# Tokens placed by expert and rank in four groups while attention and the first expert tiles run

## The reference

```python
x = x + xattn(layernorm(x), ctx, ctx)      # x, ctx: 16 batches x 256 tokens x 256
# gates = [q, k, v] @ kernel + bias; log_D = cumsum(log_sigmoid(f)) differences + i, causal
# D = exp(log_D - rowmax); C = (q k^T / sqrt(32)) * D; h = C / max(|sum C|, exp(-rowmax)) @ v
# 8 heads of 32; then layernorm over each head, times outnorm_weight
x = x + ffn(layernorm(x), w12, w3, gate_w)
# scores = x @ gate_w^T; top 2 of 8 experts, softmax over the two
# hidden = silu(x w1_e^T) * (x w2_e^T); y = sum over the two of prob * hidden @ w3_e^T
```

## Time and profile before

| what | value |
|---|---|
| median of 3 runs | 655.55 us (653.4 to 657.51) |
| the profiled execution | 654.9 us, span 653.1 us, mean granted clock 0.933 |
| busy share PE / PEld / DVE / ACT / POOL | 86% / 71% / 69% / 53% / 45% |
| DMA | 73.44 MB, mean 112 GB/s |

### The profile page before, as it was taken

How to read it: one execution, slowest core, us unless ns; L and a number is a source line. 1 busy time by engine, 2 the same in 40 slices (tenths; PEclk the granted TensorE clock), 3 DMA queues, 4 the chain that set the end, 5 groups by cost and what they waited for, 6 DMA issues and landing times.

```text
span 653.1 us, 14222 instructions
## 1 busy us (share of the span) xinstructions
PE 564.8 (86%) x3612; PEld 466.0 (71%) x3613; DVE 451.9 (69%) x987; ACT 348.5 (53%) x769; POOL 296.5 (45%) x312
## 2 busy tenths in 40 slices
PE   3779879999989951239999999999999999999993
PEld 1334668888878840127888888888888888888882
DVE  4664586787777778946667677667767767767762
ACT  2456556777777755014555555555555555555551
POOL 5423136365455534032555555555555555555532
PEclk9899998999999955559999999999999999999998
DMA  7875336787776668921433333333333333433322
GB/s 231 252 225 162 91 93 185 200 212 197 210 219 172 193 161 244 279 50 17 66 50 50 62 51 50 62 52 50 62 52 50 59 54 49 59 55 49 59 40 24
DMA packets 66018, 73.44 MB, mean 112 GB/s; under 512 B 12762, under 2 KB 55776, under 8 KB 65984
## 3 DMA queue, kind: packets, MB, share of 16 engines
q0 software_dynamic: 18240, 28.17, 25.1%
q1 hardware_dynamic: 38528, 36.21, 19.1%
q10 hardware_dynamic: 9216, 8.65, 3.9%
HBM read 43.51 MB, written 19.01 MB: 96 GB/s over the span
## 4 chain that ended last, share of the span: by engine, by line
issue 40%; POOL 15%; PE 14%; DVE 14%; DMA 10%; ACT 4%; SPq 1%; ACTq 0%; DVEq 0%; POOLq 0%
POOL xg L1168 9%; DMA out_rows<-ys,index 6%; PE bank L1287 5%; POOL out_rows L1177 4%; PE dots L1269 3%; DVE ohn L996 2%; DMA w12h<-in_x 2%; DVE ohp L995 2%; DVE c L846 1%; DVE st L727 1%; PE dots L1222 1%; ACT x2n L636 1%; PE bank L1336 1%; PE dots L1220 1%; DVE tot L887 1%
## 5 line engine op out<-in xcount | busy, mean ns | idle before, releaser
L1177 POOL DMA_INDIRECT out_rows<-ys,index x71 | 112.5, 1585 | 156.1 <-DVE ys L1048 145.1
L1054 DVE TENSOR_TENSOR w3l<-w,w3h 128x1024 fp32r<-128x1024 f32 x71 | 87.2, 1229 | 30.9 <-issue 29.7
L1168 POOL DMA_INDIRECT xg<-token_table,index x71 | 70.4, 992 | 46.1 <-DVE index L1013 24.4
L693 ACT CAST w3h<-w 128x1024 fp32r x71 | 74.4, 1048 | 20.4 <-issue 20.4
L1409 PE MATMUL bank<-w3l,hth 128*128 128x256 f32 x284 | 76.5, 302 | 1.8 <-DVE w3l L1054 1.8
L1410 PE MATMUL bank<-w3h,hth 128*128 128x256 f32 x284 | 70.8, 282 | 0.0
L1287 PE MATMUL bank<-aug,c 128*128 128x99 f32 (+2 forms) x512 | 63.9, 279 | 6.0 <-DVE c L846 5.9
L1287 PEld LDWEIGHTS bank<-aug,c 128*128 128x128 f32 x512 | 60.8, 195 | 11.0 <-DVE c L846 10.3
L1048 DVE TENSOR_SCALAR ys<-bank,pc 128x256 f32<-128x256 f32 x71 | 34.4, 484 | 46.6 <-PE bank L1413 46.6
L1031 DVE TENSOR_TENSOR htl<-bank,hth 128x512 fp32r<-128x512 f32 x71 | 49.1, 692 | 25.2 <-ACT hth L683 25.2
L1381 PE MATMUL weighs<-w12l,xh 128*128 x144 | 62.3, 432 | 1.1 <-DVE xl L1020 1.1
(11 more groups left out here) (172 smaller groups left out, 1235.1 us busy)
## 6 DMA issues: line engine op xcount, KB each, us to landing
w12l<-in_w12T SPq DMA_DIRECT2D x24, 256.0 KB, 3.5
aug<-in_ctxv SPq DMA_DIRECT2D x16, 264.0 KB, 3.5
w12h<-in_x SPq DMA_DIRECT2D x16, 256.0 KB, 3.6
w12l<-in_ctxT SPq DMA_DIRECT2D x16, 256.0 KB, 3.6
qbd<-w12h SPq DMA_DIRECT2D x64, 64.0 KB
x<-in_x SPq DMA_DIRECT2D x16, 256.0 KB, 3.3
out_rows<-x ACTq DMA_DIRECT2D x16, 256.0 KB, 2.5
token_table<-x2n ACTq DMA_DIRECT2D x16, 256.0 KB, 3.5
```

Of the source, the lines that this page charges most:

```text
L693: nc.scalar.copy(W3H[i][:], w3[:, bass.ds(e, 1)].rearrange("p a k d -> p (a k d)")).then_inc(w3h_ready, 1)
L1054: v.tensor_tensor(W3L[i][:], w3[:, bass.ds(e, 1)].rearrange("p a k d -> p (a k d)"), W3H[i][:].bitcast(F32), ALU.subtract).then_inc(w3l_re ...
L1168: q.indirect_dma_start(out=XG[x][:], out_offset=None, in_=table, in_offset=bass.IndirectOffsetOnAxis(ap=index[:, j:j + 1], axis=0)).then_i ...
L1177: q.indirect_dma_start(out=out, out_offset=bass.IndirectOffsetOnAxis(ap=index[:, j:j + 1], axis=0), in_=YS[o][:], in_offset=None, compute_ ...
```

## The change: what it does

- The tokens are routed in four groups of batches (0 to 2, 3 to 6, 7 to 11, 12 to 15). A group's top two, ranks (by matmul, with the counts of earlier groups) and slots are computed at the end of VectorE's steps two to four after the group's last batch. A slot is (expert, rank), at a fixed place of a table in memory, `slot_table`. GpSimd writes a token's number and probability there by one indirect DMA per block and choice (`place`): 64 of 128 x 8 bytes. 28 are in attention, 36 in the expert tiles, at most one or two a tile after the first.
- Three lists of tiles (21, 20 and 30) are made from it: counts, row numbers, an indirect read of up to 32 table rows (`fetch_list`), three transposes on TensorE, and copies to `index`, `prob`, `etab`, `clear`. The first list needs seven batches and is made in step 15, the second at tile 16, the third at tile 33. The one-hot products go.
- Instructions on VectorE: `largest` 6 for the first choice and 5 for the second, `chosen` 4, `take_ranks` 1 or 2, `slots` 3, `chances` 3; for a list `counts` 7 (13 the first time), `list_rows` 8 and `take_list` 6. `ranks` is 8 to 12 small matmuls.
- The rest of attention's rows (the last two batches' residual, normalisation and scores, the last group's routing) is done in tiles 0 to 11 (`remains`).
- VectorE's row statistics come after the second `combine` of a step, and scores, routing and `free_low` after them. SP loads the values ahead of the residual rows. The squares get a buffer of their own.
- All 16 steps are written out, as are the first 36 tiles (on VectorE all).
- The eight late pieces of w12 are split in steps 4 to 8, two a step: one low part by accumulating DMA, one on VectorE. Those of the last three batches are subtracted on VectorE.
- w3 isn't kept in SBUF: SP loads 512 KB for each tile into one of two buffers, two tiles ahead, once `w3l` has freed it. The register loads of the expert on ScalarE and VectorE, and `pc`, go.
- The slot table is filled early by a copy from memory to memory (264 KB).

The hunks below, after the constants: SP's loads in the expert tiles, ScalarE's `remains`, VectorE's steps and `remains`, GpSimd's placements and lists, TensorE's steps and `remains`.

```diff
+GROUPS = ((0, 3), (3, 7), (7, 12), (12, B))
+CUTS = (7, 12, B)
+FULL = [-(-(c * S * TOPK - NE * (P - 1)) // P) for c in CUTS[:2]]
+LISTS = ((0, FULL[0]), (FULL[0], FULL[1]), (FULL[1], TILES))
...
+    def load_w3(j, i):
+        wait(sp, w3l_ready, j - 1)
+        e = sp.value_load(etab[0:1, bass.ds(j, 1)], min_val=0, max_val=NE - 1)
+        sp.dma_start(W3[i][:], w3T[:, bass.ds(e * (KH * E), KH * E)]).then_inc(w3_in[i], 16)
...
+    sp.wait_ge(tables, 1)
+    load_w3(0, 0)
+    load_w3(1, 1)
+    load_rows(B - 1, 1)
+    for j in range(UNROLLED):
+        if j + 2 == FULL[0]:
+            sp.wait_ge(tables, 2)
+        load_w3(j + 2, j % 2)
+        if j == 0:
+            sp.sem_inc(may_add, 1)
+        elif j < 3:
+            sp.wait_ge(y_added[1 - j % 2], 16)
+            sp.sem_inc(may_add, 1)
+        else:
+            order(j, j % 2)
...
+        if j == 0:
+            turned(B - 3)
+        if j == 1:
+            squares(B - 1)
+        if j in (2, 5, 9):
+            nc.scalar.preload_act_table_set("natural_log_exp_and_others")
+        if j == 2:
+            row_scales(B - 2)
+            head_scales(B - 1)
+        if j == 3:
+            normal_rows(B - 2)
+            store_rows(B - 2)
+        if j == 4:
+            turned(B - 2)
+        if j == 5:
+            row_scales(B - 1)
+        if j == 6:
+            normal_rows(B - 1)
+            store_rows(B - 1)
+        if j == 7:
+            turned(B - 1)
+        if j == 9:
+            odds(len(GROUPS) - 1)
...
+    for b in range(B):
+        i = b % 2
+        if has(b, 1):
+            far(b - 1)
+        combine(b, 0)
+        if b == 2:
             columns(1, bank[7])
+        if has(b, 1):
+            centre(b - 1)
+        for gr, (lo, hi) in enumerate(GROUPS[:-1]):
+            if b == hi + 4:
+                take_ranks(gr, RANKS)
+        combine(b, 1)
+        if b == B - 1:
+            take_list(0, RANKS)
+        if b == 0:
             preactivation(1)
             maxima(1)
+        if has(b, 1):
+            variances(b - 1)
+        if has(b, 2):
+            row_statistics(b - 2)
+        if b == 1:
             three_parts(dve, v, negM, REST, m_parts, 2 * PARTS - 1, 0, PARTS)
+        if has(b, 3) and b < B - 1:
+            take_scores(b - 3, SCORES)
+        for gr, (lo, hi) in enumerate(GROUPS[:-1]):
+            if b == hi + 2:
+                largest(gr, 0)
+            if b == hi + 3:
+                largest(gr, 1)
+                chosen(gr)
+            if b == hi + 4 and b < B - 1:
+                slots(gr)
+        if has(b, 2):
+            row_means(b - 2)
+        for gr in range(2):
+            if b == GROUPS[gr][1] + 4:
+                chances(gr)
+        if b == GROUPS[1][1] + 5:
+            counts(0)
+        if b == GROUPS[1][1] + 6:
+            list_rows(0)
+        if FREE_AT < b <= FREE_AT + FREE_STEPS:
+            free_low(b - FREE_AT - 1)
...
+        if j == 0:
+            slots(2)
+            chances(2)
+            centre(B - 1)
+        if j == 1:
+            take_scores(B - 3, bank[7][:, 0:NC * NE])
+            row_statistics(B - 2)
+        if j == 2:
+            variances(B - 1)
+            counts(1)
+        if j == 3:
+            mix(B - 1)
+        if j == 4:
+            row_statistics(B - 1)
+        if j == 5:
+            take_scores(B - 2, bank[7][:, 0:NC * NE])
+            list_rows(1)
+        if j == 8:
+            take_scores(B - 1, bank[7][:, 0:NC * NE])
+            largest(3, 0)
+        if j == 9:
+            largest(3, 1)
+            chosen(3)
+        if j == 10:
+            take_ranks(3, FINAL)
+            slots(3)
+        if j == 11:
+            chances(3)
+        if j == 16:
+            take_list(1, bank[7])
+        if j == 20:
+            counts(2)
+        if j == 21:
+            list_rows(2)
+        if j == 33:
+            take_list(2, bank[7])
+    last_low(B - 3)
+    last_low(B - 2)
+    take_scores(B - 4, SCORES)
+    last_low(B - 1)
     low(0, 0)
+    far(B - 1)
+    take_ranks(2, RANKS)
...
+    def place(g, lo, hi):
+        k0 = group(g)[2]
+        pool.wait_ge(slots_ready, g + 1)
+        pool.wait_ge(pairs_ready, g + 1)
+        for k in range(k0 + lo, k0 + hi):
+            q.indirect_dma_start(out=places, out_offset=bass.IndirectOffsetOnAxis(ap=slot[:, k:k + 1], axis=0),
+                                 in_=pairs[:, k, :], in_offset=None).then_inc(placed, 16)
+    def fetch_list(ph):
+        w = LANES
+        pool.wait_ge(row_ready, 2 * ph + 2)
+        pool.wait_ge(placed, 16 * TOPK * NC * CUTS[ph])
+        q.indirect_dma_start(out=listed[0:w].rearrange("p s c -> p (s c)"), out_offset=None, in_=place_rows,
+                             in_offset=bass.IndirectOffsetOnAxis(ap=rowid[0:w, ph:ph + 1], axis=0)
+                             ).then_inc(list_in, 16)
...
+        if b in (8, 9, 10):
+            place(0, 4 * (b - 8), 4 * (b - 7))
+        if b == 11:
+            place(1, 0, 2)
+        if b in (12, 13):
+            place(1, 5 * b - 58, 5 * b - 53)
+        if b == 14:
+            place(1, 12, 16)
...
+        if j == 0:
+            place(2, 0, 4)
+        if 1 <= j < 4:
+            place(2, 2 * j + 2, 2 * j + 4)
+        if 4 <= j < 14:
+            place(2, j + 6, j + 7)
+        if j == 14:
+            fetch_list(1)
+        if 15 <= j < 31:
+            place(3, j - 15, j - 14)
+        if j == 31:
+            fetch_list(2)
...
+        for gr, (lo, hi) in enumerate(GROUPS[:-1]):
+            if b == hi + 4:
+                pe.wait_ge(kvb_ready, HG * (b + 1))
+                ranks(gr, bank[6][:, 384:512])
+        if has(b, 3):
+            turn_rows(b - 3)
+        if b == 2:
+            pe.wait_ge(o1_taken, 2)
+            columns(1, bank[7])
+        exponents(b, i, 1)
+        values(b, i, 0)
+        scores_(b, i, 1)
+        pe.wait_ge(kvb_ready, HG * (b + 1))
+        if b == B - 1:
+            pe.wait_ge(rank_taken, 2)
+            turn_list(0, bank[6][:, 384:512])
...
+    def remains(j):
+        if j == 0:
+            turn_rows(B - 3)
+        if j == 1:
+            route(B - 3, bank[7], 0)
+        if j == 4:
+            pe.wait_ge(score_ready, B - 2)
+            turn_rows(B - 2)
+        if j == 5:
+            route(B - 2, bank[7], 0)
+        if j == 7:
+            pe.wait_ge(score_ready, B - 1)
+            turn_rows(B - 1)
+        if j == 8:
+            route(B - 1, bank[7], 0)
+        if j == 10:
+            pe.wait_ge(score_ready, B)
+            ranks(3, FINAL)
+        if j == 16:
+            pe.wait_ge(rank_taken, 4)
+            turn_list(1, bank[7])
+        if j == 33:
+            pe.wait_ge(tables, 2)
+            turn_list(2, bank[7])
+        if j == UNROLLED - 1:
+            pe.wait_ge(tables, 3)
     pe.wait_ge(tables, 1)
+    route(B - 4, bank[6], NH * DV)
+    pe.wait_ge(o0_taken, B)
+    rows(0, 0)
     pe.wait_ge(w_lo, W1)
     for i in range(2):
+        pe.wait_ge(added[i], ADDED[i])
+    pe.wait_ge(free_added, 16 * FREE_STEPS)
+    pe.wait_ge(free_lo, FREE_STEPS)
+    pe.wait_ge(last_lo, SOLO)
+    pe.wait_ge(score_ready, B - 3)
+    ranks(2, bank[6][:, 384:512])
```

1039 lines of the change are left out of this document (551 added, 488 removed).

## The result

The changed kernel takes 689.73 us (median of four, 679.14 to 694.67) against 655.38 (653.40 to 657.51) before. The ratio is 1.043, with a 95% interval of 1.030 to 1.055: slower, where 628 was forecast. Kernels that carry the routing in attention scatter by 2% from run to run, so of these a median is read with its range, and a profile by its landmarks.

What follows compares the result with a forecast made beforehand. Attention was taken as a chain with TensorE in most links, the expert tiles as TensorE busy without a break. Tile 0 at 249.0 + 6.65 + 338.3 + 15 + 17.9 = 626.9, plus 1.8: 628.7, said as 628; range 610 to 646.

Steps and rivals of the forecast that it cites:

- the attention end moves by -10 + 19 + 1.4 + 1 = +11.4: Attention: new order, VectorE's additions, rank products and the slot table's early copy together move its end to 237.8 us.
- I take -10: Attention: row statistics moved into VectorE's idle time ahead of `tot` save 10 us; bounds 0 to -13.4, or -18.
- The routing on VectorE, "+16" of the +19: Attention: routing instructions lengthen VectorE's steps, 48 x 0.25 = 12.0 plus 21 x 0.207 = 4.3 us.
- The late pieces: Attention steps 4 to 8: weight-piece casts and negation on ScalarE 0, at worst 6; VectorE's `free_low` subtractions 3.0 us.
- The first list's 2.5: Attention step 15: list fetch behind the last four placements delays `turn_list` and values by 2.5 us (0 to 5).
- The handover's sum: Attention's end to tile 0: VectorE's work 8.7 plus 2.5 for the first list, 11.2 us, tile 0 at 249.0.
- The tiles' +15: Expert tiles: moved routing and remaining rows add 15 us by the largest engine excess per tile; bounds 6 and 26.
- The clock: Rival, attention: TensorE's pauses drop its clock to 1.2 GHz, five half steps 3.1 us longer; 643 us; chance 0.12.
- The W3 ring: Rival, expert tiles: 512 KB W3 loads land later than 6.75 us and lengthen all tiles; 669 us; chance 0.07.
- GpSimd becomes the bound: Rival: placements at 1.9 us cost +13 in attention, +5 in tiles, expert changes hold adds; 646 us; chance 0.15.
- More is hidden: Rival: tile additions cost 6, first list comes in time, new order gives 18; 612 us; chance 0.16.
- The rule on the port: Attention: by the skill's VectorE-GpSimd lock, each of 28 placements could wait out a VectorE instruction; nothing in the sum.

Runs made afterwards that it cites:

- b_dve: Kernel before, in its own order, with 81 small unused VectorE instructions (stand-ins for the routing) added in attention steps 5 to 15; 675.6 us.
- a_old: Changed kernel with attention's order taken back to that of before, rows' mean ahead of the routing; routing, placements and late pieces stay; 676.4 us.
- a_k: a_old_mid with TensorE's rank product behind the second scores and the late weight pieces one a step ahead of ScalarE's row scales; 670.0 us.
- a_nb: Changed kernel with the rows' mean (`nb`) moved directly behind the row statistics, ahead of the routing's instructions; 686.3 us.
- a_old_mid: a_old with the early placements behind their step's mix, ahead of the state's input, instead of at the step's end; 668.7 us.
- b_order: Kernel before with only the new order: row statistics behind the second product, ScalarE's row scales behind the head scales; 663.7 us, ratio 1.012.
- b_place64: Kernel before with only 64 plain GpSimd scatters of 8 bytes a row added, 28 in attention and 36 in expert tiles; 677.5 us.

## Why the prediction was wrong, step by step

**The step that failed** is "the attention end moves by -10 + 19 + 1.4 + 1 = +11.4". It moved by +56.5. Two of its terms are now measured apart. *"I take -10" for the new order* is +7.7. The idle 1.18 us of VectorE was real, but it was no slack for the statistics: put there, they make ScalarE's `x2n` late, and ScalarE, whose queue I did not follow past `nb`, then holds `tot`. For instructions that nobody waits for it was slack, as b_dve shows. *The routing on VectorE, "+16" of the +19* for 69 instructions, comes out in the old order (19.4 for the stand-ins, 72 of which count), but by two errors that cancel: 27.3 us of instructions, longer than I had them, less what hides in idle time. In the new order the stand-ins cost 43 to 44. That nothing hides there is what the prediction itself says ("the idle time is then spent"); it lacked the longer form beside GpSimd's mix and the clock.

Order and stand-ins together, without a placement or a weight piece, end at 276 to 277 of the 281.6. This is not 51 of the 56.5 us explained, since the parts don't add up (taking the late pieces away gives 8.0, moving `nb` 17.5). And the stand-ins are stretched more often than the real routing. In the changed kernel the routing's 72 instructions from step 4 to the last product are busy 22.3 us, where I had 16.3 with their gaps, and the four `free_low` 4.3 for 3.0; only 14 of the 72 took over 0.4, against 46 of the stand-ins. In the old order the two prices measured apart, 19.4 for the additions and 20.2 for the placements, make 39.6, and a_old, which has both and the rest, ends 37.5 later than before.

**The other terms of attention.** The late pieces, "taken at 0, at worst 6" on ScalarE and 3 on VectorE: 8.0 when left out of the changed kernel, give or take the scatter, so the bounds held and the middle did not. `ranks` waiting for `kvb` was not changed by itself; its two waits are 9.4 us together in the changed kernel, far over my +1.4, but a_k, in which the rank product stands elsewhere, was no faster. GpSimd in attention: 3 us for 28 placements in the new order, which fits "it stays level", but 20.2 in the old one. The first list's 2.5 is hidden when attention is slow and is 6.7 when it is not (a_nb).

**What held, and what was luck.** The placement took 1.35 for 1.3, and W3 landed after 3.8, under the 6.75 that costs nothing. The handover's sum, 11.9 for 11.2, is in part luck. The 2.5 for the first list were not there; in their place VectorE waited for ScalarE's cast of one of the last weight pieces, and its subtraction took 1.75 instead of 0.69:

```profile
290.88 1.75 DVE L1099 TENSOR_TENSOR w12l<-w12l,w12h 128x512 fp32r<-128x512 f32 x1 [1.82 <-ACT w12h L689]
```

The tiles' +15 was meant for all of them and is 26. That tiles 0 to 10 alone take 16.0 over is luck too: they hold waits for the landing of adds, as the 3.80 above, which I had at nothing, and in the kernel with the old order 6 of their 18.4 go with the W3 loads.

**The rivals.** *The clock* was a right mechanism, with a chance of 0.12 and 15 us for five half steps, far too few: a mean of 0.84 from 110 to 230 us is some 38 of 120 us at 1.2 GHz. It comes with the waits: behind 3.12 and 1.64 us of them, and behind 5.07, the next values took 3.71 and 3.63. By the section of the Trainium skill that I cited (TensorE: Matmul & The Clock Gate), idle gaps take the clock back; the trace agrees, with 0.84 over attention against 1.00. *The W3 ring* had the right load and the wrong place: the tiles hardly wait for W3's landing, yet its loads cost 18 to 21 us. *GpSimd becomes the bound* is false in the tiles without W3 loads, where 36 placements cost 0.0; in attention its sign, statistics waiting for `x`, came in the old order at 1.35 per placement, not 1.9. *More is hidden* is false, and its sum was wrong: an order worth 18 instead of 10 gives 8, not 5, so 608 and not 612. My bound of 0 for the order's term shut out a loss, and I had given no reason for that.

**The rule on the port.** Where I cited the Trainium skill (SBUF — State Buffer, "Who interferes with whom") for an exclusive lock between VectorE and GpSimd, I asked only whether GpSimd's descriptors wait, though a lock can hold either side. These runs show VectorE's side: its small instructions wait for GpSimd's mix (0.22 against 0.60; 3.80 for one on 16 elements). The trace of the kernel before had shown it: five of the 13 `wabs` and seven of the 13 `wden`, on 16 elements, take 0.39 to 0.73 there instead of 0.17 to 0.32.

**Open.** Why moving `nb` gave 17.5 us in the changed kernel and 1.3 with stand-ins for the routing, how much of the 45 us in attention each part causes, and what share the clock has in it, is not settled. The handover of 59 us that the change removes is worth that only if attention stays whole: 225.1 at its end and 18.6 us to tile 0's `hd`, as in the profiled run, would put tile 0 at 243.7. The best version run (a_old_mid, 668.7) is still 1.8% slower than before.

## What to carry to other kernels

Idle time of one engine inside a loop of four is no slack until each queue has been followed once around: move one instruction and read what each other engine does next. The same idle time took in some 8 us of instructions that nobody waits for (b_dve) and nothing of the statistics, which ScalarE waits for (b_order). Price an added instruction beside what will run at that moment on the engine that shares its memory path, not by its length elsewhere. A load that lands in time can still cost: W3's loads did in the tiles that also had placements and many changes of expert, and not in the others. A median can hide that two kernels differ in how many of their instructions are stretched, and not in how much: sort them by what runs beside them.

## What the runs showed of the hardware that I had not expected

VectorE's `scalar_tensor_tensor` and `tensor_scalar` of 64 elements from SBUF took 0.60 us (median) beside GpSimd's `tensor_tensor`, against 0.22 and 0.20 apart from it; `tensor_reduce` of the same size kept 0.22 (at most 0.221 in 81, nearly all beside the mix). Single instructions on 16 elements took up to 3.80, the whole length of six GpSimd instructions in a row. A plain indirect write of 8 bytes a row costs GpSimd 1.05 us and 0.30 to the next (0.98 in b_place64), almost as much as the gather of 1 KB a row (1.07). The add's landing went from 3.8 to 5.8 us in the changed kernel, with 512 KB more a tile; from 380 to 480 it is 5.5 there and 4.3 without these loads. The load itself took 3.8.
